# A four-layer kernel: a new order at the head of a first-phase step, and the state's share of a chunk's output made with tokens on partitions

## The reference

```python
def _mamba2(u, ...):                       # u = rmsnorm(x), inner width 256, state 128, 4 heads of 64
    zxbcdt = u @ in_proj_w.T               # z (256) | xBC (256 + 128 + 128) | dt (4)
    dt  = softplus(zxbcdt[..., -4:] + dt_bias)
    xBC = silu(causal_conv4(xBC) + conv_b) # xs, Bm, Cm
    dA  = exp(dt * -exp(A_log))
    def step(h, inp):                      # over the 1024 tokens
        h = dA_t * h + dt_t * x_t * B_t
        y = einsum('bhpn,bn->bhp', h, C_t)
    y = (ys + D * xs) * silu(z)
    return rmsnorm(y) * norm_w @ out_proj_w.T
x = x + mixer_scale * _mamba2(rmsnorm(x))
x = x + mlp_scale * (silu(h @ gate_w.T) * (h @ up_w.T)) @ down_w.T   # h = rmsnorm(x), hidden 512
```

## Time and profile before

| | |
|---|---|
| time, median of 3 runs | 1643.79 us (1634.2 to 1643.9) |
| the profiled execution | 1639.0 us, of which the span from first to last instruction is 1637.3 us |
| granted TensorE clock, mean | 0.904 |
| busy over the span: PE, DVE, ACT, POOL | 1378.8 us (84%), 1116.4 (68%), 852.5 (52%), 314.6 (19%) |
| first phase (slots 0 to 5) | 0 to 664 us |
| second phase | 664 to 1637.3 us |

### The profile page before, as it was taken

How to read it: one execution, slowest core, us unless ns; L and a number is a source line. 1 busy time by engine, 2 the same in 40 slices (tenths; PEclk the granted TensorE clock), 3 DMA queues, 4 the chain that set the end, 5 groups by cost and what they waited for, 6 DMA issues and landing times. The chain is left out here.

```text
span 1637.3 us, 20851 instructions
## 1 busy us (share of the span) xinstructions
PE 1378.8 (84%) x7344; PEld 615.8 (38%) x7344; DVE 1116.4 (68%) x2089; ACT 852.5 (52%) x1656; POOL 314.6 (19%) x444
## 2 busy tenths in 40 slices
PE   4778797889788877799999999999999999983560
PEld 2454473557355655122222333223332233322240
DVE  5647658565856555878888888888888888833115
ACT  5226214421532230277777777777777777772125
POOL 3221313122221301000000020141103211043351
PEclk9779998979889887589999999999999999996795
DMA  3070000020011247301111001111001100000224
GB/s 113 2 174 14 1 1 13 5 90 1 1 50 45 27 52 172 128 1 21 21 20 21 17 22 21 21 46 38 14 8 31 31 1 2 2 6 24 58 83 154
DMA packets 45965, 63.53 MB, mean 39 GB/s; under 512 B 8706, under 2 KB 33869, under 8 KB 44022
## 3 DMA queue, kind: packets, MB, share of 16 engines
q1 hardware_dynamic: 42790, 57.97, 14.6%
q0 software_dynamic: 3072, 4.23, 0.8%
HBM read 33.07 MB, written 31.15 MB: 39 GB/s over the span
## 5 line engine op out<-in xcount | busy, mean ns | idle before, releaser
L578 PE MATMUL ps<-space 128*32 128x512 f32 (+5 forms) x4608 | 860.3, 480 | 31.9 <-DVE smax L2048 7.6
L2048 DVE TENSOR_REDUCE smax<-ps 128x1 f32<-128x1024 f32 x512 | 605.2, 1220 | 116.1 <-PE ps L578 109.9
L1322 ACT ACTIVATE space<-ps 128x512 f32<-128x512 f32 x1024 | 555.5, 595 | 231.8 <-PE ps L578 231.1
L578 PEld LDWEIGHTS ps<-space 128*32 128x32 f32 (+5 forms) x4608 | 254.4, 110 | 614.2 <-ACT space L1322 329.2
L1420 POOL TENSOR_SCALAR eps_sum<-mv 128x4 f32<-128x4 f32 x32 | 7.3, 229 | 640.9 <-DVEq L1688 640.5
L578 PE MATMUL ps<-w_exp,space 128*128 128x128 f32 x512 | 86.2, 323 | 0.0
L1782 DVE SCALAR_TENSOR_TENSOR space<-space,conv_w 128x512 f32<-128x512 f32 x96 | 80.7, 850 | 4.2 <-ACT space L1151 1.6
L578 PEld LDWEIGHTS ps<-w_exp,space 128*128 128x128 f32 x512 | 74.1, 225 | 16.5 <-issue 16.5
L1198 ACT ACTIVATE btok<-ps 128x128 f32<-128x128 f32 x32 | 8.9, 277 | 135.1 <-DVE Gm L1800 68.8
L1530 POOL DMA_INDIRECT expert_in<-space,slot x64 | 62.9, 982 | 37.6 <-issue 19.3
L1902 DVE TENSOR_TENSOR space<-xnT,ps 128x512 f32<-128x512 f32 x64 | 42.1, 683 | 31.0 <-PE ps L578 31.0
(11 more groups left out here) (246 smaller groups left out, 1457.3 us busy)
## 6 DMA issues: line engine op xcount, KB each, us to landing
q_rows<-space SPq DMA_DIRECT2D x24, 256.0 KB, 2.5
k_rows<-space SPq DMA_DIRECT2D x24, 256.0 KB, 2.8
space<-k_rows SPq DMA_DIRECT2D x16, 384.0 KB, 5.2
space<-q_rows SPq DMA_DIRECT2D x16, 384.0 KB, 6.8
expert_out<-x_all SPq DMA_DIRECT2D x2, 2048.0 KB, 20.4
space<-expert_out SPq DMA_DIRECT2D x4, 1024.0 KB, 8.8
v_rows<-space SPq DMA_DIRECT2D x4, 668.0 KB, 3.6
space<-v_rows SPq DMA_DIRECT2D x4, 668.0 KB, 6.5
```

The costliest lines, as they stand in the source:

```text
L578: return nc.tensor.matmul(out, lhsT, rhs, start=first, stop=last)
L1322: nc.scalar.activation(prob[:, QUAD * (step % PROB_SETS) + unit % QUAD, :], bank(STB + unit % 2), ACT.Exp)\
L2048: v.tensor_reduce(smax[:, N % 2, i:i + 1], ps[:, b0:b0 + 2, :].rearrange("p k n -> p (k n)"), AX.X, ALU.max).then_inc(S.s_max, 1)
```

## The change

In the head of a step: DVE calls `rms_apply` before `convolve(0)`; between `convolve(1)` and the loop stands only the first half of `expert_norm(q)`; in the loop comes `hidden(0)`, then its second half, then after each `hidden(n)` with n = 1..6 one `convolve(n+1)`; `tail_norm` stands at n = 4. `skip_rows` goes from POOL to DVE, behind the loop. ACT copies projections 2 and 3 out without their taps, loads the SiLU table, copies the turned MLP input out, and makes the two taps then. ACT also loads the Exp table right behind the last convolution's SiLU. `xinT` lies where `Cs` was. (A slot without p has no MLP: there DVE's order stays as it was.)

In the chunks: PE multiplies C (stationary) by the whole carried state in one 128x256 matmul (`chunk_carried`), so that the result has tokens on partitions; DVE scales each token's row by its decay (`chunk_scaled`, 128x256, which comes from one more sum in `decay_sums` and a wider `decay`), and `chunk_out` turns and adds it by two matmuls with the identity in place of the four with the state. `chunk_spread`, its exponential and `chunk_outer` are gone. PE's order is carried(c), state(c), front(c+1), after(c+1), out(c); DVE's is carry(c), scaled(c), inputs(c+1), weights(c+1).

```diff
             def decay_sums(b):
-                for i, m in enumerate((after, ones)):
+                for i, m in enumerate((after, ones, upto)):
...
-            def chunk_spread(b, c):
-                pe.wait_ge(S.l_ready, 2 * (NT * b + c) + 1)
-                mm(bank(SEGB), ones[:], aU[:, c % 2].rearrange("p h n -> p (h n)")).then_inc(S.seg_psum, 1)
+            def chunk_carried(b, c):
+                pe.wait_ge(S.h_ready, NT * b + c + 1)
+                if b + c > 0:
+                    pe.wait_ge(S.yt_ready, NT * b + c)
+                if c == 0 and b >= 1:
+                    pe.wait_ge(S.mix_var, 2 * b)
+                mm(bank(STUB)[:, D_INNER:2 * D_INNER], tile(xbc[:, 3], c), hst[:, c % 2].rearrange("p h d -> p (h d)"))\
+                    .then_inc(S.yi_psum, 1)
             def chunk_out(b, c):
-                pe.wait_ge(S.cs_ready, NT * b + c + 1)
-                pe.wait_ge(S.h_ready, NT * b + c + 1)
-                for h in range(SSM_HEADS):
-                    mm(out, xdt[:, c % 2, h], Wm[:, c % 2, h], True, False)
-                    last = mm(out, hst[:, c % 2, h], Cs[:, c % 2, h], False, True)
+                pe.wait_ge(S.yt_ready, NT * b + c + 1)
+                for j in range(2):
+                    for h in range(2):
+                        mm(out[...], xdt[:, c % 2, 2 * j + h], Wm[:, c % 2, 2 * j + h], True, False)
+                    last = mm(out, ytok[:, c % 2, 2 * j:2 * j + 2]..., ident[:], False, True)
             # PE's loop
-                    chunk_spread(m, 0)
                 for c in range(NT):
+                        chunk_carried(m, c)
                         if c < NT - 1:
                             chunk_state(m, c)
                             chunk_front(m, c + 1)
...
                         chunk_out(m, c)
-                            chunk_spread(m, c + 1)
             # ACT's loop
-                    for i in range(4):
+                    for i in range(2):
                         evac_projection(m, i)
                         tap(m, i)
+                    for i in range(2, 4):
+                        evac_projection(m, i)
                 if p is not None:
+                    table_of(ACT.Silu, 0)
                     evac_T("mlp", p, (5, 6))
+                if m is not None:
+                    for i in range(2, 4):
+                        tap(m, i)
...
                     silu_conv(m, N_CONV - 1)
+                table_of(ACT.Exp, 1)
...
-                    chunk_exp(m, 0, 0)
-                    chunk_exp(m, 0, 1)
+                    chunk_exp(m, 0)
             # DVE
-            def chunk_outer(b, c):
-                v.tensor_tensor(Cs[:, c % 2], xbc[:, 3, c * P:(c + 1) * P]..., EL[:, c % 2, 1], ALU.mult)
+            def chunk_scaled(b, c):
+                dve.wait_ge(S.yi_psum, NT * b + c + 1)
+                v.tensor_tensor(ytok[:, c % 2], bank(STUB)[:, D_INNER:2 * D_INNER]...,
+                                decay[:, 2, c].unsqueeze(2).to_broadcast([P, SSM_HEADS, SSM_DIM]), ALU.mult)
             # DVE's loop
                     step_sizes(m)
-                    convolve(m, 0)
                 if p is not None:
                     for H in range(2):
                         rms_apply(p, H)
                 if m is not None:
+                    convolve(m, 0)
                     convolve(m, 1)
                 if q is not None:
-                    for H in range(2):
-                        expert_norm(q, H)
-                if m is not None:
-                    convolve(m, 2)
+                    expert_norm(q, 0)
+                    if p is None:
+                        expert_norm(q, 1)
                 for n in range(2 * HID_TILES):
-                    if m is not None and n in (0, 3, 4, 5, 6):
-                        convolve(m, 3 if n == 0 else n + 1)
                     if p is not None:
                         hidden(p, n)
-                    if q is not None and n == 2:
+                    if q is not None and p is not None and n == 0:
+                        expert_norm(q, 1)
+                    if m is not None and 1 <= n <= N_CONV - 2:
+                        convolve(m, n + 1)
+                    if q is not None and n == 4:
                         for H in range(2):
                             tail_norm(q, H)
+                if p is not None:
+                    skip_rows(p)
...
-                        chunk_inputs(m, c + 1)
                         chunk_carry(m, c)
+                        chunk_scaled(m, c)
+                        chunk_inputs(m, c + 1)
                         chunk_weights(m, c + 1)
-                        if c < HT:
-                            chunk_outer(m, c + 1)
```

More of the change, by code:

```diff
@@ L236, in build @@
         rstd3 = sb("rstd3", [P, NT])
+        warm = sb("warm", [P, 2])
         o_rec = sb("o_rec", [P, HT, QUAD])
@@ L635, in chunk_after @@
                 if c >= 1:
[L636 removed]
+                    pe.wait_ge(S.l_ready, NT * b + c)
                 mm(bank(SEGB), after[:], aU[:, c % 2].rearrange("p h n -> p (h n)")).then_inc(S.seg_psum, 1)
[L639 to L642 removed]
             def chunk_state(b, c):
[L646 to L647 removed]
                 pe.wait_ge(S.xw_ready, (NT - 1) * b + c + 1)
@@ L661, in chunk_out @@
                 pe.wait_ge(S.w_ready, NT * b + c + 1)
-                pe.wait_ge(S.cs_ready, NT * b + c + 1)
-                pe.wait_ge(S.h_ready, NT * b + c + 1)
-                for h in range(SSM_HEADS):
-                    lo = SSM_DIM * (h % 2)
-                    out = tile(bank(YB), 2 * (h // 2) + c % 2)[lo:lo + SSM_DIM]
-                    mm(out, xdt[:, c % 2, h], Wm[:, c % 2, h], True, False)
-                    last = mm(out, hst[:, c % 2, h], Cs[:, c % 2, h], False, True)
+                pe.wait_ge(S.yt_ready, NT * b + c + 1)
+                for j in range(2):
+                    out = tile(bank(YB), 2 * j + c % 2)
+                    for h in range(2):
+                        mm(out[SSM_DIM * h:SSM_DIM * h + SSM_DIM], xdt[:, c % 2, 2 * j + h], Wm[:, c % 2, 2 * j + h], True, False)
+                    last = mm(out, ytok[:, c % 2, 2 * j:2 * j + 2].rearrange("p h d -> p (h d)"), ident[:], False, True)
                 last.then_inc(S.y_psum, 1)
@@ L1125, in decays @@
                     act.wait_ge(S.hdec_ready, (NT - 1) * b)
-                nc.scalar.activation(decay[:].rearrange("p s c h -> p (s c h)"), bank(TRB)[:, 0:64], ACT.Exp)\
+                    act.wait_ge(S.yt_ready, NT * b)
+                nc.scalar.activation(decay[:].rearrange("p s c h -> p (s c h)"), bank(TRB)[:, 0:96], ACT.Exp)\
                     .then_inc(S.decay_exp, 1)
@@ L1198, in chunk_copy, with chunk_exp @@
                 nc.scalar.activation(btok[:, c % 2], bank(TRB)[:, 2 * P:3 * P], ACT.Copy).then_inc(S.btok_ready, 1)
-            def chunk_exp(b, c, k):
-                act.wait_ge(S.seg_psum, 2 * (NT * b + c) + k + 1)
+            def chunk_exp(b, c):
+                act.wait_ge(S.seg_psum, NT * b + c + 1)
                 if c >= 2:
-                    act.wait_ge(*((S.w_ready, NT * b + c - 1), (S.cs_ready, NT * b + c - 1))[k])
-                nc.scalar.activation(EL[:, c % 2, k].rearrange("p h n -> p (h n)"), bank(SEGB), ACT.Exp).then_inc(S.l_ready, 1)
+                    act.wait_ge(S.w_ready, NT * b + c - 1)
+                nc.scalar.activation(EL[:, c % 2].rearrange("p h n -> p (h n)"), bank(SEGB), ACT.Exp).then_inc(S.l_ready, 1)
             def gated_squares(b, pair):
@@ L1254, in _ @@
                         chunk_copy(m, c + 1)
-                        chunk_exp(m, c + 1, 0)
+                        chunk_exp(m, c + 1)
                     if p is not None and c == HT:
                         evac_gates(p)
-                    if m is not None and c < NT - 1:
-                        chunk_exp(m, c + 1, 1)
                     if m is not None and c in (2, 4, 6):
@@ L1466, in chunk_decays @@
                                 ALU.mult).then_inc(S.hdec_ready, 1)
-            def skip_rows(b):
-                pool.wait_ge(S.x1_ready, 2 * b + 2)
-                if b >= 1:
-                    pool.wait_ge(S.normed, 6 * b - 4)
-                g.tensor_tensor(xa[:], xin[:, b % 2], x1[:], ALU.add).then_inc(S.res_sum, 1)
             input_root(0)
@@ L1491, in _ @@
                 if p is not None:
-                    skip_rows(p)
                     for H in range(2):
@@ L1867, in hidden, with skip_rows @@
                 v.tensor_tensor(hidT[:, f, half(H)], silu_g[:, n % 2], bank(mlp_bank(2 * n + 1)), ALU.mult).then_inc(S.hid_ready, 1)
+            def skip_rows(b):
+                if b >= 1:
+                    dve.wait_ge(S.normed, 6 * b - 4)
+                mine.wait(mine.n)
+                v.tensor_tensor(xa[:], xin[:, b % 2], x1[:], ALU.add).then_inc(S.res_sum, 1)
             def skip_sum(b, H):
@@ L1985, in _ @@
                     chunk_weights(m, 0)
-                    chunk_outer(m, 0)
                 if q is not None:
@@ L1993, in _ @@
```

(10 more changed lines are left out.)

50 lines of the change are left out of this document (25 added, 25 removed).

## The result

The changed kernel takes 1611.4 us (median, 1605.1 to 1620.7) against 1639.3 us of the kernel before beside it: ratio 0.9847, 95% interval 0.9812 to 0.9882. The forecast was 1596 with a range of 1581 to 1618. The sign came true and the time lies in the range; the gain is 28 us in the medians and 32.9 us between the two profiled executions (spans 1637.3 and 1604.4 us), where I had worked out 44.3. The measured time is nearer to the rival in which only the head pays (1619) than to the forecast.

What follows compares the result with a forecast made beforehand. DVE was taken to bound the head of a step, and a chain round PE, ACT and DVE the chunks. Heads 20.9 and chunks 23.4, together 44.3 us off 1640.2, gave 1596 us, range 1581 to 1618.

Steps and rivals of the forecast that it cites:

- the rival in which only the head pays: Whole kernel: the chunks are worth 0 and only the heads gain, giving 1619 us; chance 0.10.
- What bounds the kernel: First phase: DVE bounds the head of a step; the chunks are a chain round PE, ACT and DVE.
- The list of DVE's steps in slots 2 and 3: Heads of slots 2 and 3: DVE followed step by step in the new order; down 7.6 and 7.7 us earlier.
- The head of slot 1: Head of slot 1: the MLP's input comes 4.7 us earlier, and down 5.6 us earlier.
- Chunks up to the gates: Slots 1 to 3, from down to the gates: shorter by 17.6 us in all.
- Slot 0: Chunks of slot 0, up to the step sizes of slot 1: shorter by 8.2 us in all.
- an interval of 6.84 us becomes 5.2: Slot 0: a chunk interval with 2.0 us of position tables in it shrinks from 6.84 to 5.2 us.
- Chunks with experts' sums: Chunks c = 4 to 7, slots 1 to 3: little gain there, a net loss of 0.8 us a slot.
- c = 4 wins 0.8, since `chunk_outer` no longer stands before the first expert input: Chunk c = 4, slots 1 to 3: 0.8 us gained with chunk_outer gone from before the first expert input.
- The two identity matmuls cost what the four with the state cost, some 0.45: chunk_out on PE: two identity matmuls cost the same as the four state matmuls, some 0.45 us.
- The rival of the clock: Chunks: without the dense spreads PE's clock falls by 0.05, some 16 us more, giving 1612 us; chance 0.10.
- Waits for `chunk_scaled` under 1 us: PE in the chunks: new waits for chunk_scaled stay under 1 us; above 2 us would show the forecast wrong.

Runs made afterwards that it cites:

- e10_skip_gpsimd: The changed kernel with skip_rows back on GpSimd at its old place in that queue; ratio 0.9946 to the kernel before.
- e11_norms_first: The changed kernel with both halves of the expert norm ahead of the first product again; ratio 0.9911 to the kernel before.
- e4_no_sums: The changed kernel with GpSimd's products aU of chunks 2 to 7 of every step left out; ratio 0.9882 to the kernel before.
- e1_head: The kernel before with only the new head order, on its old chunks; ratio 0.9874 to the kernel before.
- e5_out_halves: The changed kernel with chunk_out's two 128-column ytok matmuls cut into four of 64 columns; ratio 0.9854 to the kernel before.
- e6_weights_late: The changed kernel with DVE's chunk_weights(c+1) behind the expert inputs from c = 4 on; ratio 0.9791 to the kernel before.
- the four edits: The changed kernel with exponential before copy, chunk_out in halves, weights late from c = 4, carried early; ratio 0.968, repeated 0.9711, to the kernel before.

## Why the prediction was right or wrong

- **The number.** 44.3 us were forecast and 32.9 came between the traces. The heads gave what I had said (20.6 for 20.9). The chunks gave 10 us of 23.4: 4.4 in slot 0 and 18.8 up to the gates, less 13.1 behind them. That the time lies in the range is owed to the width that I left for such losses, not to the terms of the chunks.
- **What bounds the kernel.** Right. The head belonged to DVE: the new order took its 20.6 us there, and alone on the old chunks 21.4.
- **The list of DVE's steps in slots 2 and 3.** The sum (7.6 and 7.7, measured 7.4 and 7.2) was right. `rms_apply` took 2.1 us for my 2.3, but the convolution behind it 3.0 for 2.3, since POOL's second aU reaches into it. The first product came 8.6 us earlier for 9. `skip_rows` took 1.22 us for 1.2, and its move was worth 5 us, as `e10_skip_gpsimd` shows. What I had not seen is that the place of the second half of the norm matters by itself: it keeps PE's stall for a product at 2.3 us at most, where `e11_norms_first` has 4.72 and the half clock behind it.
- **The head of slot 1.** 6.0 for 5.6. No drain behind the table load shows, as the row said. But "hidden by PE's turning" was wrong: the turning ends at 124.1 us, the load stands from 123.69 to 124.97 ahead of the copy on ACT, and PE waits 1.61 us for that copy, nearly all of its idle time in this head.
- **Chunks up to the gates.** Right: 18.8 for 17.6 us. The interval from c = 3 to 4 in slots 2 and 3 went from 5.65 to 4.65 us, the full microsecond that I had forecast.
- **Slot 0.** Wrong, 4.4 for 8.2 us. The failed step is "an interval of 6.84 us becomes 5.2": it became 5.75. I let `chunk_weights` meet aU, but not the position casts behind it. aU no longer waits for the spread, and where the cast has aU beside it, it costs 0.84 us more. `e4_no_sums` gives 4.4 us, some of which POOL already took before (the third cast of a chunk took 1.05 us there for 0.69). This is one half of what lacks: the seven intervals between the `chunk_inputs` of slot 0 gave 6.5 us together. The other half is the end of the slot, at which I hadn't looked: from the last `chunk_inputs` to the step sizes of slot 1 it takes 21.6 us for 19.6. Two of the longer `chunk_out` lie there, and `mix_out(0)` stands 0.61 us for `chunk_scaled(7)`. The head alone has 19.6 there, no sums 21.6, the halves 20.4.
- **Chunks with experts' sums.** Behind the gates I had put +0.8 us a slot; at the same clock it is about +2.1 in slots 1 and 2, and +2.9 in slot 3 (80.5 us against 77.6 of `e1_head`, both at 0.87). The changed kernel against the old chunks (of before and of `e1_head`): between the gates and the sixth `chunk_inputs` 3.0 and 2.35 us, because carry and scaled now stand ahead of it; sixth to seventh 13.4 and 13.5 at 0.75; seventh to eighth (c = 5) 10.25 and 10.0 at 1.00; from the eighth to the next step (c = 6 and 7) 30.2 and 28.9 at 0.94, 31.7 and 30.5 at 0.89. For c = 5, 6 and 7 together that is +1.5, and I had said +1.6. The term that failed is "c = 4 wins 0.8, since `chunk_outer` no longer stands before the first expert input": it loses 0.6. In its place DVE's carry, scaled, the 0.88 us for the exponential and the weights stand before `evac_parts` (L1904), for which PE now stands 1.15 us; with the weights late 0.26 us of that were left.
- **`chunk_out`.** "The two identity matmuls cost what the four with the state cost, some 0.45" is wrong: 1.15 us became 1.65 (the 1.08 in the expectation of `e5_out_halves` ends with the start of the next matmul). In c = 5 it cost nothing on top, since the wait behind it (0.72) would have been 1.22 otherwise; at the end of slot 0 the halves are worth 1.2 us. The loss of c = 5 came in the size forecast, and in c = 7 came a wait that I had not named: `mix_out(0)` writes into the PSUM bank from which `chunk_scaled(7)` reads, is ordered behind it, and stands 0.61 us.
- **The rest, some 6 of 13 us behind the gates, stays open.** It is a remainder, 13.1 less 2.1, 2.1 and 2.9. 4.2 us of the 13 lie between the sixth and the seventh `chunk_inputs` (42.8 us in three slots against 38.6), and nearly all of that in slot 3, where the clock is 0.65 and was 0.94. But over all that stands behind the gates the granted clock has the same mean in both traces, 0.88 (0.86, 0.91, 0.87 against 0.90, 0.85, 0.88). So the clock isn't lower on the whole. If it has a part in the remainder, it is by where its half level falls, and that isn't shown. The rival of the clock (0.10) reasoned by the dense spreads that go and by a clock 0.05 lower over the chunks. It didn't come true: from `down` to the next step the clock is 0.91, 0.92, 0.91 and was 0.95, 0.88, 0.89.
- **Waits for `chunk_scaled` under 1 us.** Wrong: 27.0 us in 21, the longest 3.3, which was one of my own signs of being wrong. Most stand up to c = 3 and in slot 0, where DVE sets the pace anyway.
- **Second phase.** 971.4 us for 973.

## What to carry to other kernels

When a matmul is replaced by one of another shape, price it with its neighbours: the same sums took 1.15 us as eight matmuls of 64 columns and 1.65 us as six of mixed width. When a step is taken away, ask what it had held back and what it had filled: here the spread had kept POOL's product away from DVE's casts and had filled PE's wait for an expert input; each small edit that repairs one of these (exponential first, weights behind the expert inputs, the carried share into the hole) looks like nothing or like 0.5% alone, and all four are 1.6% under the changed kernel. And keep PE's stalls short: splitting 5.2 us of DVE work in two around a product was worth 2.5 us a step, though DVE had the same work, because PE ran at half the clock behind the longer stall. Last, compare a stage at the same granted clock before a loss is put down to the code, and look at the mean clock before it is put down to the clock.

## What was unexpected in the hardware

- A matmul with 128 columns of weights between pairs of 64 columns costs 0.42 us a start, where the same one as two of 64 costs 0.22, and a pair of 64 ahead of it 0.37 instead of 0.22 to 0.27. In the kernel before, the last pair, with a matmul of 128 columns behind it, took 0.37 too (378.31 to 378.68). The reason for it isn't shown.
- After a stall of PE of 1.65 us, half the clock followed in slot 1 of `e6_weights_late` (0.50 from 187.8 to 197.9 us) with no second stall behind it. After the same stall with the four edits it didn't, in six of six. What tells the two apart isn't shown.
- An ACT table load of 1.28 us was followed by the next ACTIVATE 0.02 us later (124.97 to 124.99 in the trace after) and 0.09 us later; the copy ahead of it ended at 123.68, 0.01 us before it.
